# An RG-LRU and ternary-FFN layer: the first w1/w3 unit of the second sequence ahead of the first down product, a gate formed bank by bank, g's between scans

## The chip, the cores and the metric

The kernel runs on one core of a Trainium2 chip. The metric is the device time of one execution in microseconds, as the median of several runs. The engines have their own instruction streams: TensorE (PE, matmuls into PSUM; PEld is its weight load), VectorE (DVE), ScalarE (ACT), GpSimd (POOL) and SyncE (SP, which issues the DMAs here). They wait for each other by semaphores alone.

## The reference, cut to what matters

Two sequences of 512 tokens of width 256 go through one layer. The output is x plus a recurrent branch plus a feed-forward branch, both of the normalised x:

```python
xn = _layernorm(x, axis=-1)
# recurrent branch
y = gelu(xn @ w_y + b_y)
xb = xn @ w_x + b_x
conv = conv_b + sum(conv_w[k] * shifted(xb, k) for k in range(4))
gate_x = sigmoid(conv @ w_ig + b_ig)
gate_a = sigmoid(conv @ w_ag + b_ag)
log_a = -8.0 * gate_a * softplus(a_param)
a = exp(log_a); mult = sqrt(1.0 - exp(2.0 * log_a))
nx = gate_x * conv * mult            # first token: a = 0, mult = 1
h[t] = a[t] * h[t-1] + nx[t]         # scan over the 512 tokens
out1 = (h * y) @ w_out + b_out
# feed-forward branch, weights made ternary: w -> {-s, 0, s}, s = mean|w|
g = silu(xn @ w1q.T) * (xn @ w3q.T)  # hidden width 682 = 5 * 128 + 42
out2 = g @ w2q.T
return x + out1 + out2
```

## The kernel before, in words

Everything stays in SBUF. Channels lie on the partitions and tokens on the free axis; a sequence s is 512 columns, and 256 channels are two chunks c. Values that meet a matmul are split into a rounded part and its rest (hi and lo, kind fp32r), so a product of 128x512 is several matmuls: hi times hi, the weight's lo times hi, and hi times the value's lo. The order on each engine is written out by hand, and every engine does its list strictly in that order.

The recurrent branch comes first. TensorE forms the products with w_x (for the convolution), w_y, and the two gates WIG and WAG for s = 0 and 1. Gate products of a sequence lie in a slot of PSUM, which is two banks of 512 columns, one for each output chunk o. The slot of the second gate of sequence 0 (GA_SLOT[0] = 0) is that in which the w_x product of sequence 1 lay (X_SLOT[1] = 0), and older_taps(1, c) on VectorE (lines 484 to 496) reads bank c of it while it forms the convolution; conv_set counts finished convolutions, two for each sequence. Before that gate product TensorE waits for all four (line 780). dense_product (line 657) works chunk by chunk over both banks.

The feed-forward branch has ten units: hidden(n) for n = 0 to 9 (line 664), n = 5 * s + j, each with eight matmuls of 512 columns for w1 and w3 at once into a slot (H_SLOT), and hidden_tail for the 42 last channels of both sequences. For each unit, ScalarE forms silu_of(n) from the slot (line 327), VectorE g_of(n) = silu * s32 * the w3 half (line 508), ScalarE its rounded part g_hi_of(n) (line 335), GpSimd the rest, lo_of_g(n), which is called g_lo(n) here (line 253). The buffers of silu and g are rings of three. The tail has the same by tail_product, tail_hi (two casts, lines 567 and 568) and tail_lo (line 573), all on VectorE.

down(s, banks, first) (line 688) multiplies g with w2: for each j it waits for g_lo, does eight matmuls of 256 columns (four token tiles, hi and lo), and after the five j's comes the tail with four. project(s, first) (line 707) multiplies the gated scan with w_out, chunk by chunk, when hy_set says that gated_output(s, c) is done; its float32 matmuls are two records each in the trace, 32 records for both sequences. Both add into the same banks, for s = 0 down first and for s = 1 project first.

The recurrence on VectorE is, for each s: gated_input (line 518), squares, gated_products (line 529, once ScalarE has formed mult by a square root, line 370), scan(s, c) for the two chunks (line 536), gated_output(s, c) (line 541). threshold_2 (line 475) forms the scale and the threshold of w2 from a sum in PSUM. ScalarE changes its table before the square roots and again before the silus of sequence 1.

Five output steps (line 547) add x, and SyncE stores each.

Of the kernel before, what the change touches and what calls it, by code (L numbers as in the profile page):

```python
# [19 lines left out]
P = 128  # L20
# [5 lines left out]
KC = D // P  # L26
TILES = SEQ // P
FULL = HIDDEN // P
# [12 lines left out]
WX, WY, WIG, WAG, WOUT = range(5)  # L41


def build(nc: bass.Bass, x, dense, w13t, w2t, params, b_out, out):
# [7 lines left out]
    with ctx:  # L52
        def sb(name, shape, dt=f32):
            return ctx.enter_context(nc.sbuf_tensor(name, shape, dt))

        def sem(name):
            return ctx.enter_context(nc.semaphore(name))
# [9 lines left out]
        w_hi = sb("w_hi", [P, 5, KC, D], f32r)  # L67
        w_lo = sb("w_lo", [P, 5, KC, D], f32r)
# [7 lines left out]
        conv_hi = sb("conv_hi", [P, SEQS, KC, SEQ], f32r)  # L76
        conv_lo = sb("conv_lo", [P, SEQS, KC, SEQ], f32r)
# [39 lines left out]
        slot = [ctx.enter_context(nc.psum_tensor(f"slot{i}", [P, 2, SEQ], f32)) for i in range(4)]  # L117
        T_SLOT, X_SLOT, Y_SLOT = (0, 1), (2, 0), (3, 1)
        GX_SLOT, GA_SLOT = (2, 3), (0, 1)
# [13 lines left out]
        def xt_bank(s, h):  # L133
# [21 lines left out]
        w_lo_set = sem("w_lo_set")  # L155
# [7 lines left out]
        tap_set, tap_step, conv_set = sem("tap_set"), sem("tap_step"), sem("conv_set")  # L163
        conv_hi_set, conv_lo_set = sem("conv_hi_set"), sem("conv_lo_set")
        y_psum, y_set = sem("y_psum"), sem("y_set")
        gx_psum, ga_psum, tx_set, ta_set = sem("gx_psum"), sem("ga_psum"), sem("tx_set"), sem("ta_set")
        a_set, a2_set, mult_set, mult0_set = sem("a_set"), sem("a2_set"), sem("mult_set"), sem("mult0_set")
        nx_step, nx_set, h_set, hy_set = sem("nx_step"), sem("nx_set"), sem("h_set"), sem("hy_set")
        h_psum, silu_set, g_set, g_hi_set, g_lo_set = (
            sem("h_psum"), sem("silu_set"), sem("g_set"), sem("g_hi_set"), sem("g_lo_set"))  # L170
# [258 lines left out]
        def _(dve):  # L429
# [34 lines left out]
            def ternary_13():  # L464
                dve.wait_ge(thr_set, 2)
                dve.wait_ge(gaps_set, 1)
                parts = (slice(0, W3_AT), slice(W3_AT, W13))
                for i, cols in enumerate(parts):
                    nc.vector.tensor_scalar(below[:, :, cols], w13_raw[:, :, cols], thr[:, 1, i:i + 1], None, ALU.is_lt).then_inc(below_set, 1)
                for i, cols in enumerate(parts):  # L470
                    dve.wait_ge(below_set, i + 1)
                    nc.vector.scalar_tensor_tensor(out=w13_q[:, :, cols], in0=w13_raw[:, :, cols], scalar=thr[:, 0, i:i + 1],
                                                   in1=below[:, :, cols], op0=ALU.is_gt, op1=ALU.subtract).then_inc(w13_q_set, 1)

            def threshold_2():
                dve.wait_ge(sum2_psum, 1)
                nc.vector.tensor_scalar(scale[:, 2:3], sum2[:, 0:1], sum2[:, 1:2], 1.0 / WEIGHTS, ALU.add, ALU.mult).then_inc(s2_ready, 1)
                nc.vector.tensor_scalar(thr2[:, 0:1], sum2[:, 0:1], sum2[:, 1:2], 0.5 / WEIGHTS, ALU.add, ALU.mult).then_inc(s2_ready, 1)
                nc.vector.tensor_scalar(thr2[:, 1:2], sum2[:, 0:1], sum2[:, 1:2], -0.5 / WEIGHTS, ALU.add, ALU.mult).then_inc(s2_ready, 1)
                dve.wait_ge(s2_ready, 1)  # L480
                dve.wait_ge(thr_set, 3)
                nc.vector.tensor_tensor(s32[:, :], scale[:, 1:2], scale[:, 2:3], ALU.mult).then_inc(scale2_set, 1)
# [25 lines left out]
            def g_of(n):  # L508
                s, j = HJ[n]
                if n == 0:  # L510
                    dve.wait_ge(scale2_set, 1)
                dve.wait_ge(silu_set, n + 1)
                if n >= RING:
                    dve.wait_ge(g_lo_set, n - RING + 1)
                nc.vector.scalar_tensor_tensor(out=g[:, n % RING], in0=silu[:, n % RING], scalar=s32[:, 0:1],  # L515
                                               in1=slot[H_SLOT[s][j]][:, 1], op0=ALU.mult, op1=ALU.mult).then_inc(g_set, 1)

            def gated_input(s):

                dve.wait_ge(tx_set, KC * (s + 1))  # L520
                nc.vector.scalar_tensor_tensor(out=tx[:, s], in0=tx[:, s], scalar=1.0, in1=conv[:, s],
                                               op0=ALU.add, op1=ALU.mult).then_inc(nx_step, 1)
# [6 lines left out]
            def gated_products(s):  # L529

                dve.wait_ge(mult0_set, 1)
                dve.wait_ge(nx_step, s + 1)
                dve.wait_ge(mult_set, KC * (s + 1))
                nc.vector.tensor_tensor(tx[:, s], tx[:, s], mult[:, s], ALU.mult).then_inc(nx_set, 1)

            def scan(s, c):

                dve.wait_ge(nx_set, s + 1)
                nc.vector.tensor_tensor_scan(tx[:, s, c], ta[:, s, c], tx[:, s, c], 0.0, ALU.mult, ALU.add).then_inc(h_set, 1)

            def gated_output(s, c):

                dve.wait_ge(y_set, KC * s + c + 1)
                dve.wait_ge(h_set, KC * s + c + 1)
                nc.vector.tensor_tensor(tx[:, s, c], tx[:, s, c], y[:, s, c], ALU.mult).then_inc(hy_set, 1)
# [53 lines left out]
            older_taps(1, 1)  # L599
            threshold_13()  # L600
            ternary_13()
            gated_input(0)
            threshold_2()
            ternary_w2()
            squares(0)
            squares(1)
# [9 lines left out]
            gated_products(0)  # L616
            scan(0, 0)
            scan(0, 1)
            gated_output(0, 0)
            gated_output(0, 1)  # L620
            gated_products(1)
            g_of(5)
            scan(1, 0)
            g_of(6)
            scan(1, 1)
            gated_output(1, 0)
            g_of(7)
            gated_output(1, 1)
            g_of(8)
            g_of(9)  # L630
            for n in range(len(O_ALL)):
                output(n)

# [2 lines left out]
        def _(pe):  # L636
# [27 lines left out]
            def hidden(n):  # L664

                s, j = HJ[n]
                for o, col in enumerate((j * P, W3_AT + TAIL + j * P)):
                    for c in range(KC):
                        for v in (xt_hi, xt_lo):
                            mm = nc.tensor.matmul(slot[H_SLOT[s][j]][:, o], w13_q[:, c, col:col + P], v[:, s, c],  # L670
                                                  start=(c == 0 and v is xt_hi), stop=(c == KC - 1 and v is xt_lo))
                mm.then_inc(h_psum, 1)
# [10 lines left out]
            def out_tile(s, i, t):  # L683

                at = (t - O_TILES[s][i].start) * D
                return O_BANK[s][i][:, at:at + D]

            def down(s, banks, first):

                for j in range(FULL + 1):  # L690
                    if j < FULL:
                        pe.wait_ge(g_lo_set, FULL * s + j + 1)
                    else:
                        pe.wait_ge(gt_hi_set, 2)
                        pe.wait_ge(gt_lo_set, 1)
                        pe.wait_ge(b_placed, 32)
                    for i in banks:
                        tiles = O_TILES[s][i]
                        for t in tiles:
                            rows = slice(t * P, (t + 1) * P)  # L700
                            parts = (g_hi[:, j], g_lo[:, j]) if j < FULL else (gt,)
                            for k, v in enumerate(parts):
                                mm = nc.tensor.matmul(out_tile(s, i, t), v[:, s, rows], w2_q[:, j], start=(first and j == 0 and t == tiles.start and k == 0),  # L703
                                                      stop=(not first and j == FULL), skip_group_check=True)
                return mm
# [63 lines left out]
            dense_terms(slot[X_SLOT[1]], WX, [(w_hi, xt_lo[:, 1])], False, True).then_inc(xb_psum, 1)  # L769
            dense_product(slot[Y_SLOT[1]], WY, xt_hi[:, 1], xt_lo[:, 1], y_psum)  # L770

            def gate_product(s, m, slots, done, between=None):
                pe.wait_ge(w_lo_set, m + 1)
                dense_product(slot[slots[s]], m, conv_hi[:, s], conv_lo[:, s], done,
                              (conv_hi_set, KC * s + 1), (conv_lo_set, KC * s + 1), between)

            pe.wait_ge(conv_set, KC)
            gate_product(0, WIG, GX_SLOT, gx_psum)
            sums_of_w13()
            pe.wait_ge(conv_set, 2 * KC)  # L780
            gate_product(0, WAG, GA_SLOT, ga_psum)
            pe.wait_ge(thr_set, 3)
            gate_product(1, WIG, GX_SLOT, gx_psum, sum_of_w2)
            pe.wait_ge(y_set, 2 * KC)
# [11 lines left out]
            hidden(3)  # L796
            pe.wait_ge(g_set, 2)
            hidden(4)
            pe.wait_ge(w2_q_set, 1)
            pe.wait_ge(g_t_set, 1)  # L800
            down(0, range(len(O_TILES[0])), True)
            pe.wait_ge(g_set, 3)
            hidden(5)
            pe.wait_ge(g_set, 4)
            hidden(6)
            pe.wait_ge(g_set, 5)
# [8 lines left out]
            for i in range(len(O_TILES[1])):  # L815
                down(1, [i], False).then_inc(o_psum, 1)
# [27 lines left out]
```

## Time and profile before

| | us |
|---|---|
| median of 3 runs | 77.18 (77.08 to 77.36) |
| profiled execution | 77.82 |
| its span, first to last instruction | 76.0 |
| TensorE matmul busy | 70.0 (92%) |
| VectorE busy | 60.8 (80%) |
| ScalarE busy | 49.9 (66%) |
| GpSimd busy | 33.4 (44%) |

The granted TensorE clock is 1.000 (of 2.4 GHz) over the span. The times in the profile count from the first instruction. Busy shares are averages over the whole span; the stage rows and the timeline rows below tell more. A timeline row shows when an instruction started and how long it lasted, and this includes time in which it had started and was held up. In the name of a tile buffer numbers are left out, and tiles that share memory carry the name of the first: g and silu lie in w_raw there, ternary weights are w_q, y lies in xn_y.

### The profile page before, as it was taken

What the parts mean: (1) busy time and instruction counts of PE and PEld (TensorE: products, weight loads), DVE (VectorE), ACT (ScalarE), POOL (GpSimd) and SP (SyncE); (2) the same over time, 40 slices, a digit from 0 to 9 for tenths busy, and PEclk for the clock granted to TensorE, in tenths of its full rate; (3) what the DMA queues carried; (4) which work ended last, traced back from release to release, by engine and by line L of the source; (5) the groups of instructions that cost most, each with busy time, mean ns of one, the idle gap of its engine ahead of it and who ended that gap; (6) DMA issues with size and microseconds to landing.
All of it is one profiled execution on the core that took longest, in us unless ns stands there. A gap on an engine that the chain in (4) does not pass through costs nothing.

```text
span 76.0 us, 1062 instructions
## 1 busy us (share of the span) xinstructions
PE 70.0 (92%) x364; PEld 60.1 (79%) x364; DVE 60.8 (80%) x99; ACT 49.9 (66%) x76; POOL 33.4 (44%) x43
## 2 busy tenths in 40 slices
PE   4999879999999799999999999499999999999960
PEld 4999768877887678888888889388888888899950
DVE  4887599999999999999989999169999999400340
ACT  3663714899999999999989768996357429100000
POOL 6385646336661750052007968940007818910000
DMA  0989999910000000000000000000000000340062
GB/s 13 259 212 338 349 405 367 361 67 9 0 0 0 4 0 0 0 0 0 5 1 0 0 9 0 0 0 0 0 0 0 0 0 0 111 165 9 0 207 69
DMA packets 5095, 5.63 MB, mean 74 GB/s; under 512 B 525, under 2 KB 4578, under 8 KB 5090
## 3 DMA queue, kind: packets, MB, share of 16 engines
q1 hardware_dynamic: 4946, 5.55, 21.8%
q8 instruction: 3, 0.05, 0.2%
q10 hardware_dynamic: 144, 0.01, 0.1%
q14 instruction: 2, 0.02, 0.1%
HBM read 4.51 MB, written 1.05 MB: 73 GB/s over the span
## 4 chain that ended last, share of the span: by engine, by line
PE 37%; ACT 33%; DVE 9%; DMA 7%; issue 5%; POOL 3%; SPq 3%; DVEq 0%; ACTq 0%
PE slot L670 12%; PE slot L703 11%; PE slot L714 9%; DMA x_sb<-x 7%; ACT ta L363 4%; POOL g_lo L256 3%; ACT tx L349 3%; ACT conv_hi L342 3%; ACT xn_y L324 3%; PE slot L653 2%; ACT ta L355 2%; SPq L186 2%; ACT g_hi L300 2%; DVE w_raw L515 2%; DVE stats L437 2%
## 5 line engine op out<-in xcount | busy, mean ns | idle before, releaser
L256 POOL TENSOR_TENSOR g_lo<-w_raw,g_hi 128x512 fp32r<-128x512 f32 x10 | 15.9, 1609 | 16.1 <-ACT g_hi L338 16.1
L670 PE MATMUL slot<-xt_lo,w_q 128*128 128x512 f32 x40 | 15.7, 394 | 0.0
L670 PE MATMUL slot<-xt_hi,w_q 128*128 128x512 f32 x40 | 15.7, 393 | 0.0
L703 PE MATMUL slot<-w_q,g_hi 128*128 128x256 f32 x40 | 10.2, 292 | 1.1 <-POOL g_lo L256 1.1
L703 PE MATMUL slot<-w_q,g_lo 128*128 128x256 f32 x40 | 9.8, 282 | 0.0
L332 ACT ACTIVATE w_raw<-slot,scale 128x512 f32<-128x512 f32 x10 | 6.8, 686 | 4.3 <-PE slot L670 4.3
L493 DVE SCALAR_TENSOR_TENSOR conv<-slot,par,conv 128x511 f32<-128x511 f32 (+2 forms) x12 | 9.0, 748 | 0.4
L703 PEld LDWEIGHTS slot<-w_q,g_hi 128*128 128x128 f32 x40 | 7.6, 191 | 1.6 <-POOL g_lo L256 1.6
L670 PEld LDWEIGHTS slot<-xt_lo,w_q 128*128 128x128 f32 x40 | 7.5, 188 | 1.7
L670 PEld LDWEIGHTS slot<-xt_hi,w_q 128*128 128x128 f32 x40 | 7.5, 188 | 1.7
L338 ACT ACTIVATE g_hi<-w_raw 128x512 fp32r<-128x512 f32 x10 | 6.3, 630 | 3.4 <-DVE w_raw L515 3.2
L552 DVE TENSOR_TENSOR x_sb<-slot,x_sb 128x512 f32<-128x512 f32 (+1 forms) x5 | 2.8, 581 | 6.8 <-PE slot L703 6.8
L703 PEld LDWEIGHTS slot<-w_q,g_lo 128*128 128x128 f32 x40 | 7.6, 191 | 0.1
L515 DVE SCALAR_TENSOR_TENSOR w_raw<-w_raw,s,slot 128x512 f32<-128x512 f32 x10 | 7.2, 740 | 0.4 <-ACT w_raw L332 0.4
L226 POOL TENSOR_TENSOR w_lo<-w_raw,w_hi 128x512 fp32r<-128x512 f32 x4 | 5.1, 1287 | 4.6 <-ACT w_hi L283 4.6
L722 PE MATMUL slot<-ones 128*128 128x128 f32 x28 | 6.2, 420 | 1.0 <-POOL ones L214 1.0
L714 PE MATMUL slot<-w_raw,tx 128*128 128x256 f32 x32 | 7.1, 379 | 0.0
L653 PE MATMUL slot<-conv_hi,w_hi 128*128 128x512 f32 x16 | 6.4, 401 | 0.5 <-DVE conv L493 0.5
L251 POOL TENSOR_TENSOR conv_lo<-conv,conv_hi 128x512 fp32r<-128x512 f32 x4 | 5.4, 1343 | 3.4 <-ACT conv_hi L342 3.4
L722 PEld LDWEIGHTS slot<-ones 128*128 128x128 f32 x28 | 6.0, 330 | 1.0 <-POOL ones L214 1.0
L714 PEld LDWEIGHTS slot<-w_raw,tx 128*128 128x128 f32 x32 | 6.1, 190 | 0.9
L653 PE MATMUL slot<-conv_hi,w_lo 128*128 128x512 f32 x16 | 6.3, 394 | 0.0
(105 smaller groups left out, 143.1 us busy)
## 6 DMA issues: line engine op xcount, KB each, us to landing
w_raw<-w13t SPq DMA_DIRECT2D x2, 682.0 KB, 8.1
w_raw<-dense SPq DMA_DIRECT2D x5, 256.0 KB, 5.7
out<-x_sb SPq DMA_DIRECT2D x3, 256.0 KB, 2.2
w_raw<-w2t SPq DMA_DIRECT2D x1, 640.0 KB
x_sb<-x SPq DMA_DIRECT2D x4, 128.0 KB, 2.2
x_sb<-x SPq DMA_DIRECT2D x1, 512.0 KB, 5.4
out<-x_sb SPq DMA_DIRECT2D x2, 128.0 KB, 1.7
w_raw<-w2t SPq DMA_DIRECT2D x2, 42.0 KB
```

The lines of the kernel that those rows point to most:

```text
L226: nc.gpsimd.tensor_tensor(w_lo[:, m], w_raw[:, m], w_hi[:, m].bitcast(f32), ALU.subtract).then_inc(w_lo_set, 1)
L251: nc.gpsimd.tensor_tensor(conv_lo[:, s, c], conv[:, s, c], conv_hi[:, s, c].bitcast(f32), ALU.subtract).then_inc(conv_lo_set, 1)
L256: nc.gpsimd.tensor_tensor(g_lo[:, j, s], g[:, n % RING], g_hi[:, j, s].bitcast(f32), ALU.subtract).then_inc(g_lo_set, 1)
L332: nc.scalar.activation(silu[:, n % RING], slot[H_SLOT[s][j]][:, 0], ACT.Silu, scale=scale[:, 0:1]).then_inc(silu_set, 1)
L338: nc.scalar.activation(g_hi[:, j, s], g[:, n % RING], ACT.Copy).then_inc(g_hi_set, 1)
L493: nc.vector.scalar_tensor_tensor(out=conv[:, s, c, i:], in0=slot[X_SLOT[s]][:, c, 0:SEQ - i], scalar=par[:, CONV_W + KC * k + c:CONV_W + K ...
L515: nc.vector.scalar_tensor_tensor(out=g[:, n % RING], in0=silu[:, n % RING], scalar=s32[:, 0:1], in1=slot[H_SLOT[s][j]][:, 1], op0=ALU.mult ...
L653: mm = nc.tensor.matmul(dst[:, o], w[:, m, c, o * P:(o + 1) * P], v[:, c], start=(first and i == 0 and c == 0), stop=(last and i == len(te ...
L670: mm = nc.tensor.matmul(slot[H_SLOT[s][j]][:, o], w13_q[:, c, col:col + P], v[:, s, c], start=(c == 0 and v is xt_hi), stop=(c == KC - 1 a ...
L703: mm = nc.tensor.matmul(out_tile(s, i, t), v[:, s, rows], w2_q[:, j], start=(first and j == 0 and t == tiles.start and k == 0), stop=(not ...
L714: mm = nc.tensor.matmul(out_tile(s, i, t), tx[:, s, c, t * P:(t + 1) * P], w_raw[:, WOUT, c], start=(first and c == 0 and t == tiles.start ...
L722: nc.tensor.matmul(slot[WARM_SLOT][:, 0, 0:P], ones[:, :], ones[:, :], start=True, stop=True)
```

## The change

There are four edits. On TensorE, hidden(5) comes before down(0) and no longer after it. The second gate of sequence 0 is formed bank by bank by a new function, gate_bank, which waits for three convolutions ahead of bank 0 and for four ahead of bank 1. The first down product takes the tail before its last j. On VectorE, threshold_2 comes before gated_input(0), and the g's of sequence 1 are put between gated products, scans and gated outputs, with gated_output(1, 0) and (1, 1) at the end.

```diff
@@ VectorE @@
             threshold_13()
             ternary_13()
+            threshold_2()
             gated_input(0)
-            threshold_2()
             ternary_w2()
...
             gated_products(0)
             scan(0, 0)
             scan(0, 1)
+            g_of(5)
+            gated_products(1)
+            g_of(6)
             gated_output(0, 0)
+            g_of(7)
             gated_output(0, 1)
-            gated_products(1)
-            g_of(5)
             scan(1, 0)
-            g_of(6)
+            g_of(8)
             scan(1, 1)
+            g_of(9)
             gated_output(1, 0)
-            g_of(7)
             gated_output(1, 1)
-            g_of(8)
-            g_of(9)
@@ TensorE @@
             def down(s, banks, first):
-                for j in range(FULL + 1):
+                order = (*range(FULL - 1), FULL, FULL - 1) if first else range(FULL + 1)
+                for j in order:
...
+            def gate_bank(s, m, slots, o):
+                terms = [(w, v, c) for w, v in ((w_hi, conv_hi), (w_lo, conv_hi), (w_hi, conv_lo)) for c in range(KC)]
+                for i, (w, v, c) in enumerate(terms):
+                    mm = nc.tensor.matmul(slot[slots[s]][:, o], w[:, m, c, o * P:(o + 1) * P], v[:, s, c],
+                                          start=(i == 0), stop=(i == len(terms) - 1))
+                return mm
...
-            pe.wait_ge(conv_set, 2 * KC)
-            gate_product(0, WAG, GA_SLOT, ga_psum)
+            pe.wait_ge(w_lo_set, WAG + 1)
+            for o in range(KC):
+                pe.wait_ge(conv_set, KC + o + 1)
+                mm = gate_bank(0, WAG, GA_SLOT, o)
+            mm.then_inc(ga_psum, 1)
...
             hidden(4)
+            pe.wait_ge(g_set, 3)
+            hidden(5)
             pe.wait_ge(w2_q_set, 1)
             pe.wait_ge(g_t_set, 1)
             down(0, range(len(O_TILES[0])), True)
-            pe.wait_ge(g_set, 3)
-            hidden(5)
```

## Rows read from the trace of the kernel before

**Rows 1.** Stages: us, busy (x instructions) of PE, PEld, DVE, ACT, POOL, clock, DMA.
```profile
45.00:52.00 7.00, 5.86 (x46) 5.45 (x45) 4.71 (x6) 6.60 (x9) 4.90 (x3) 1.00 0.00 0
52.00:61.00 9.00, 9.00 (x41) 7.29 (x40) 9.00 (x10) 4.50 (x7) 3.27 (x2) 1.00 0.00 0
```
**Rows 2.** The chain of waits that ended last: start us, us, what.
```profile
46.72 2.30 POOL g_lo L256
...
52.01 9.26 PE slot L670 x40
```
**Rows 3.** Timeline, TensorE at its two waits: start us, us, instruction, idle before and releaser.
```profile
24.34 0.28 PE L736 MATMUL slot<-abs_sum,ones 128*128 128x2 f32 x2
25.15 0.50 PE L653 MATMUL slot<-conv_hi,w_hi 128*128 128x512 f32 x1 [0.53 <-DVE conv L493]
...
49.07 0.38 PE L703 MATMUL slot<-w_q,g_hi 128*128 128x256 f32 x1 [1.11 <-POOL g_lo L256]
```
**Rows 4.** TensorE, first and last: 24 of down(0), 40 of hidden(5) to (9), projections.
```profile
44.92 0.28 PE L703 MATMUL slot<-w_q,g_hi 128*128 128x256 f32 x1
...
47.67 0.28 PE L703 MATMUL slot<-w_q,g_lo 128*128 128x256 f32 x1
...
51.85 0.40 PE L670 MATMUL slot<-xt_hi,w_q 128*128 128x512 f32 x1
...
60.88 0.39 PE L670 MATMUL slot<-xt_lo,w_q 128*128 128x512 f32 x1
61.11 7.07 PE L714 MATMUL slot<-w_raw,tx 128*128 128x256 f32 x32
```
**Rows 5.** ScalarE: silu_of(3) and g_hi_of(2).
```profile
43.27 0.69 ACT L332 ACTIVATE w_raw<-slot,scale 128x512 f32<-128x512 f32 x1 [0.52 <-PE slot L670]
43.85 0.62 ACT L338 ACTIVATE g_hi<-w_raw 128x512 fp32r<-128x512 f32 x1
```
**Rows 6.** VectorE: g_of(2), the two casts of the tail, and tail_lo.
```profile
42.86 0.75 DVE L515 SCALAR_TENSOR_TENSOR w_raw<-w_raw,s,slot 128x512 f32<-128x512 f32 x1
43.64 0.83 DVE L567 CAST gt_hi<-w_raw 42x1024 fp32r<-42x1024 f32 x1
44.51 0.69 DVE L568 CAST gt<-w_raw 42x1024 fp32r<-42x1024 f32 x1
...
46.67 1.22 DVE L573 TENSOR_TENSOR gt<-w_raw,gt_hi 42x1024 fp32r<-42x1024 f32 x1
```
**Rows 7.** GpSimd: g_lo(0) and (1), g_lo(2), g_lo(3) and (4).
```profile
40.45 3.47 POOL L256 TENSOR_TENSOR g_lo<-w_raw,g_hi 128x512 fp32r<-128x512 f32 x2 [5.73 <-ACT g_hi L338]
44.55 1.81 POOL L256 TENSOR_TENSOR g_lo<-w_raw,g_hi 128x512 fp32r<-128x512 f32 x1 [0.63 <-ACT g_hi L338]
46.72 3.54 POOL L256 TENSOR_TENSOR g_lo<-w_raw,g_hi 128x512 fp32r<-128x512 f32 x2 [0.36 <-ACT g_hi L338]
```
**Rows 8.** VectorE: gated_output(0,0) and (0,1); scan(1,0), g_of(6), scan(1,1), gated_output(1,0).
```profile
53.63 1.27 DVE L545 TENSOR_TENSOR tx<-tx,xn_y 128x512 f32<-128x512 f32 x2
...
56.61 1.22 DVE L539 TENSOR_TENSOR_SCAN tx<-ta,tx 128x512 f32<-128x512 f32 x1
57.74 0.72 DVE L515 SCALAR_TENSOR_TENSOR w_raw<-w_raw,s,slot 128x512 f32<-128x512 f32 x1
58.38 1.61 DVE L539 TENSOR_TENSOR_SCAN tx<-ta,tx 128x512 f32<-128x512 f32 x1
59.92 1.72 DVE L545 TENSOR_TENSOR tx<-tx,xn_y 128x512 f32<-128x512 f32 x1
```
**Rows 9.** GpSimd: g_lo(5) and g_lo(6).
```profile
57.43 1.48 POOL L256 TENSOR_TENSOR g_lo<-w_raw,g_hi 128x512 fp32r<-128x512 f32 x1 [7.18 <-ACT g_hi L338]
59.21 1.88 POOL L256 TENSOR_TENSOR g_lo<-w_raw,g_hi 128x512 fp32r<-128x512 f32 x1 [0.30 <-ACT g_hi L338]
```
**Rows 10.** gated_products(0) on VectorE, and ScalarE's table load before silu_of(5).
```profile
50.08 1.25 DVE L534 TENSOR_TENSOR tx<-tx,mult 128x1024 f32<-128x1024 f32 x1 [2.19 <-ACT mult L370]
...
51.20 1.28 ACT L332 ACT_TABLE_LOAD   x1
```

## The prediction

> **What bounds the kernel now.** I read the stage table first. TensorE is busy for the whole of 52 to 61 us and VectorE is too; only 45 to 52 us has TensorE time missing (5.86 of 7 us), at a granted clock of 1.00 [rows 1]. The chain of waits then says which of the two sets the end: from 52.01 us it is TensorE alone, first 9.26 us of w1/w3 units [rows 2], then projections and the last down product. So before the change TensorE ends last, and VectorE, as busy, is a step behind it. How far behind is what matters here: the scanned output of the second sequence (gated_output(1,0), called hy3 below) is ready at 59.92 + 1.72 = 61.64 us [rows 8], while project(1), which reads it, begins at its place 17 of 32 records from 61.11 us, 61.11 + 16 x 0.2155 = 64.56 us (0.2155 is (67.8 - 61.11)/31, 7.07 us for 32 records less the 0.38 us that one lasts) [rows 4]. VectorE has 2.9 us of slack there, and nothing else reaches the end by another way.
>
> TensorE's own idle time is in two places: 0.53 us before the second gate product of the first sequence, and 1.11 us before j = 3 of the first down product, which waits for GpSimd's g_lo(3) [rows 3].
>
> **Part 1, the gate bank by bank.** The wait for all four convolutions becomes one for three, then four. The last record of the sums starts at about 24.45 us (two of them, 0.28 us long, from 24.34) and the gate could not start before 25.15, where its first record also lasts 0.50 us in place of the usual 0.39 [rows 3, 4]. After the change the six products of bank 0 start at about 24.68; bank 1 then wants the fourth convolution 1.4 us later, when it is long there. The same 12 matmuls, nothing added: TensorE is s = 0.58 us earlier from here. I bound s by 0.4 (the wait alone, less queueing) and 0.65. It survives to the w1/w3 units because threshold_2 goes ahead of gated_input(0): without that the constants that hidden(0) waits for would come a gated_input later, some 1.2 us (the same shape takes 1.25 [rows 10]); the two steps only change places, so their own cost on VectorE is nil (0 to 0.1).
> ScalarE gets nothing from s for now: it works through its own list without a gap that TensorE causes until silu(3), which waited 0.52 us for it at 43.27 us [rows 5].
>
> **Part 2, hidden(5) before down(0).** Eight matmuls of 0.2315 us ((60.88 - 51.85)/39) are 1.85 us [rows 4]. With s, hidden(5) runs 44.33 to 46.18, down(0) starts there, and its first 24 products (0.1196 us each, (47.67 - 44.92)/23 [rows 4]) end at 49.05. If g_lo(3) still came at 49.02 [rows 2] and g_lo(4) at 50.26 [rows 7], both waits would be gone (the tail's four products now lie before j = 4), hidden(6) would start at 51.45 in place of 53.70, and project(1) at 62.3.
>
> **Part 3, where that collides.** g_lo(3) will not come at 49.02. The rows show that a VectorE instruction with two inputs in SBUF, or a cast from SBUF to SBUF, and a GpSimd tensor_tensor never run together: the later one waits to the end of the other. Three cases: g_lo(6) starts at 59.21, the scan ends at 59.99, g_lo(6) ends 1.10 us after that; gated_output(1,0) is next on VectorE at 59.92 but GpSimd was waiting first, so it ends 0.55 us after g_lo(6) (alone it takes 0.67) [rows 8, 9]. g_lo(3) starts 0.05 us behind tail_lo (46.67 + 1.22 = 47.89) and ends 1.13 us after it [rows 2, 6]. And cast 1 of the tail (43.64) stands until g_lo(1) is through at 43.92, ends at 44.47; cast 2 follows at 44.51, g_lo(2) at 44.55, 0.04 us late, and it waits for the cast until 45.20 [rows 6, 7].
> That last race turns. silu(3) comes up to s earlier, so g_hi(2) starts when g_of(2) is done (42.86 + 0.75, and 0.04) and not at 43.85, where silu(3) let it in [rows 5, 6]; g_lo(2) asks at 43.65 + 0.62 + 0.08 = 44.35, while cast 1 runs, and is first at 44.48. It ends at 45.63, cast 2 at 46.19 in place of 45.20. VectorE is 0.99 us late, and with it g_of(3), g_of(4), tail_lo, ScalarE's g_hi(4), table load and four square roots, and gated_products(0), which starts at 51.07 in place of 50.08 [rows 10]. An s of 0.05 us is enough for this, so its bounds do not matter. g_lo(3) ends at 50.00, g_lo(4) at 51.24: TensorE waits 1.0 us before j = 3 after all, j = 3 and the tail run to 51.59, j = 4 to 52.55. hidden(6) to hidden(9) are 32 x 0.2315 = 7.41, to 59.96; project(0), 3.45, to 63.41. TensorE is 1.15 us ahead of before.
>
> **Part 4, VectorE's new order.** It now has g_of(8) and g_of(9) ahead of hy3. A step starts 0.08 us before the one ahead of it ends, so undisturbed it adds to that end: gated_products 1.14 (1.22 or 1.25 long), scan 1.13, g_of 0.66, gated_output 0.60 [rows 8, 10]. Behind a GpSimd hold a scan ends 1.08 after it (58.38 + 1.61 against 57.43 + 1.48), a gated_output 0.55 [rows 8, 9]. GpSimd asks 0.04 + 0.63 + 0.08 = 0.75 us after each g_of ends. That is what makes the spread order dear: behind every g_of stands a VectorE step that needs the shared access, and g_lo lands on it. I walk it.
> scan(0,0), scan(0,1) end at 54.70 (silu(5) is there at 54.17, its table loaded 0.99 late [rows 10]). g_of(5) to 55.35. gated_products(1) to 56.49; g_lo(5) asks at 56.09, gets 56.49 to 57.60. g_of(6) to 57.15; gated_output(0,0) waits to 57.60, ends 58.15. g_lo(6) asks at 57.89, holds to 59.27. g_of(7) to 58.81; gated_output(0,1) ends at 59.82. g_lo(7) asks at 59.59 (its g_hi stands behind silu(8), which ends at 58.98), before scan(1,0) does (59.74), holds to 60.94; scan(1,0) ends at 62.02. g_of(8) to 62.68; scan(1,1) to 63.81, which g_lo(8) waits for and holds to 64.90. g_of(9) to 64.47; gated_output(1,0) ends at 64.90 + 0.55 = 65.45: hy3. g_lo(9) comes before gated_output(1,1), which ends at 67.12; project(1) wants that one 8 x 0.2155 after its start, 67.2 us.
> TensorE is ready at 63.41, so it waits 2.1 us and starts project(1) at 65.50 where it was 64.56, with about 0.1 us for the first product after a wait (0.38 us at 49.07 for one of 0.28 [rows 3, 4]). Sum: +0.94 + 0.10 = +1.0 us. Everything behind it is as before: g_lo(9) at 66.6 is long there when the last down product comes to it, and the stores of the first sequence are issued by 68.5 us, four us ahead of the last.
> The bounds of this step: the walk holds 2.3 us of collisions ahead of hy3 (0.4, 0.4, 1.1, 0.4); with none of them hy3 comes at 63.2, TensorE is not held, and the change is worth -1.15; with one more collision than I count (1.1 us) +2.1. I take the walk, since each of its waits repeats one in the rows. The new waits stall no other queue: ScalarE's silu(9) is done at 60.84, no DMA is moved.
>
> The Trainium skill ("SBUF — State Buffer", on the two sides of SBUF) says that VectorE and GpSimd share a port pair as an exclusive lock, that an instruction with two SBUF inputs or in a two-port mode takes it, and that who starts first keeps it for the whole instruction. It also names the intuition it replaces, bandwidth shared in proportion. By the lock the walk stands; by sharing, overlaps would stretch both sides a little and the time would lie nearer the no-collision end. The trace agrees with the lock: 1.72 us for a 0.67 us step, ending 0.55 after the other's end [rows 8, 9].
>
> **From the profile's time to the median.** The profiled run took 77.82 us for a span of 76.0; the median of the runs is 77.18, so I add the difference of spans, 1.0, to 77.18: **78.2 us**.
>
> **Rivals.**
> A. The forecast, +1.0: chance 0.52. Its own range is 77.8 to 78.7.
> B. g_lo(7) asks just after scan(1,0). The margin is 0.15 us (59.59 against 59.74), and it hangs on silu(8), which waits for TensorE. The scan then runs first, gated_output(1,0) ends at 64.75, project(1) starts at 64.80: +0.24 + 0.10 = +0.3, 77.5 us. Chance 0.14.
> C. The race at 44.5 us does not turn (the g_lo(2) request comes later than I work out by 0.16 us). Then everything on VectorE is 0.99 earlier, with the same collisions: hy3 at 64.45, project(1) at 64.50, TensorE idle from 62.3: -0.06 + 0.10, 77.2 us, no change. Chance 0.14.
> D. The other side: TensorE stays the bound. Its mechanism is the refilled stall and s, at the price of -1.15 us with the race turned (76.0) and -2.3 without (74.9). It decides from the point where VectorE has hy3 before 64.1 us: that is faster by 0.5%, and it wants the collisions ahead of hy3 to cost under 0.9 us and not 2.3 (under 1.9 if the race doesn't turn). For it: the kernel before paid only 1.5 us in all there (0.40 on scan(1,1), 1.05 on gated_output(1,0) [rows 8]), and had 2.9 us of slack. Against it: the new order puts a locked step behind each of the five g_of's. Chance 0.20.
>
> **How the numbers follow.** A change of 0.5% (0.39 us) is about what a measurement of this kernel tells from none. Slower by more: A and a little of B, 0.54. Within: most of B, and C, 0.25. Faster: D and the edge of C, 0.21. The range reaches from D's first value, 76.0, to 78.6; outside are D without the race (about 0.08) and a further collision (0.08).
>
> **What would show it.** Right: gate products start near 24.7 us; silu(3) without a wait; g_lo(2) about 1.15 us long from cast 1's end and cast 2 over 1.5 us long; no TensorE gap at hidden(5), one of about 1 us before j = 3; VectorE with both gated outputs of sequence 0 and scan(1,0) lengthened; a TensorE gap of about 2 us before project(1), and a chain of waits that runs through VectorE and GpSimd in 55 to 65 us. Wrong: a project(1) that follows project(0) without a gap (D), or cast 2 at 0.69 us (C). A granted clock under 1.00 behind the longer gap would add to A; no gap in the trace of before is that long.

## The result, and the profile after

| | before | changed |
|---|---|---|
| median (range), us, 4 runs each | 77.25 (77.08 to 77.36) | 79.62 (78.85 to 79.78) |
| ratio, 95% interval | | 1.029 (1.022 to 1.036) |
| profiled execution, its span | 77.82, 76.0 | 79.61, 77.8 |
| granted clock of the changed kernel's 4 executions | | 1.000, 0.978, 1.000, 0.978 |

The changed kernel is 2.9% slower. The forecast was slower, 78.2 us, with an upper end of 78.6: the direction came as forecast, the size did not. Three more sets of six executions on other occasions gave ratios of 1.015, 1.020 and 1.022; what differs between them is shown below. (Ratios set aside executions over 1.5% above the fastest of their kernel, which here took out neither of the two with a low clock; wherever a low clock matters, I give all executions.)

The stages of the profile after, columns as in [rows 1]: TensorE now has its hole in 61 to 68 us (4.92 of 7), while VectorE is busy for all of it.

```profile
45.00:52.00 7.00, 6.01 (x43) 5.47 (x42) 4.71 (x6) 5.02 (x7) 4.81 (x3) 1.00 0.01 2
52.00:61.00 9.00, 9.00 (x46) 7.55 (x45) 8.96 (x10) 6.84 (x11) 3.79 (x3) 1.00 0.00 0
61.00:68.00 7.00, 4.92 (x23) 4.05 (x22) 7.00 (x7) 1.73 (x3) 3.48 (x3) 1.00 0.00 0
```

Everything in this trace is 0.57 us late from the start, since the statistics of the second sequence waited longer for the load of x. VectorE's timeline at that place, before and after:

```profile
8.49 0.43 DVE L437 BATCH_NORM_STATS2 stats<-x_sb 128x6 f32<-128x256 f32 x1 [1.06 <-DMA x_sb<-x]
```
```profile
9.06 0.75 DVE L437 BATCH_NORM_STATS2 stats<-x_sb 128x6 f32<-128x256 f32 x2 [1.53 <-DMA x_sb<-x]
```

Take 0.57 off and the lines can be laid beside the forecast. The gate products start right behind the sums:

```profile
25.06 0.71 PE L777 MATMUL slot<-conv_hi,w_hi 128*128 128x512 f32 x2
```

That is 24.49 on the old clock where it was 25.15, so s is 0.66 us (forecast 0.58, bound 0.65). The race of [rows 5 to 7], ScalarE, VectorE and GpSimd after the change:

```profile
44.24 0.63 ACT L338 ACTIVATE g_hi<-w_raw 128x512 fp32r<-128x512 f32 x1 [0.32 <-DVE w_raw L515]
```
```profile
44.24 0.82 DVE L567 CAST gt_hi<-w_raw 42x1024 fp32r<-42x1024 f32 x1
45.09 1.72 DVE L568 CAST gt<-w_raw 42x1024 fp32r<-42x1024 f32 x1
```
```profile
44.95 1.30 POOL L256 TENSOR_TENSOR g_lo<-w_raw,g_hi 128x512 fp32r<-128x512 f32 x1 [0.45 <-ACT g_hi L338]
```

It turned: g_lo(2) asks at 44.38 on the old clock (forecast 44.35), goes first, and cast 2 takes 1.72 us for its 0.69. VectorE's list behind it, then GpSimd's g_lo(5) to g_lo(8) (compare [rows 8, 9]):

```profile
57.03 0.74 DVE L515 SCALAR_TENSOR_TENSOR w_raw<-w_raw,s,slot 128x512 f32<-128x512 f32 x1
57.69 1.13 DVE L545 TENSOR_TENSOR tx<-tx,xn_y 128x512 f32<-128x512 f32 x1
58.74 0.73 DVE L515 SCALAR_TENSOR_TENSOR w_raw<-w_raw,s,slot 128x512 f32<-128x512 f32 x1
59.40 1.12 DVE L545 TENSOR_TENSOR tx<-tx,xn_y 128x512 f32<-128x512 f32 x1
60.45 2.29 DVE L539 TENSOR_TENSOR_SCAN tx<-ta,tx 128x512 f32<-128x512 f32 x1
62.66 0.72 DVE L515 SCALAR_TENSOR_TENSOR w_raw<-w_raw,s,slot 128x512 f32<-128x512 f32 x1
63.30 1.21 DVE L539 TENSOR_TENSOR_SCAN tx<-ta,tx 128x512 f32<-128x512 f32 x1
64.43 0.72 DVE L515 SCALAR_TENSOR_TENSOR w_raw<-w_raw,s,slot 128x512 f32<-128x512 f32 x1
65.07 1.05 DVE L545 TENSOR_TENSOR tx<-tx,xn_y 128x512 f32<-128x512 f32 x1
```
```profile
56.72 1.55 POOL L256 TENSOR_TENSOR g_lo<-w_raw,g_hi 128x512 fp32r<-128x512 f32 x1 [4.84 <-ACT g_hi L338]
58.52 1.46 POOL L256 TENSOR_TENSOR g_lo<-w_raw,g_hi 128x512 fp32r<-128x512 f32 x1 [0.24 <-ACT g_hi L338]
60.22 1.44 POOL L256 TENSOR_TENSOR g_lo<-w_raw,g_hi 128x512 fp32r<-128x512 f32 x1 [0.24 <-ACT g_hi L338]
64.12 1.46 POOL L256 TENSOR_TENSOR g_lo<-w_raw,g_hi 128x512 fp32r<-128x512 f32 x1 [2.46 <-ACT g_hi L338]
```

Both gated outputs of sequence 0 are 0.45 us too long, scan(1,0) 1.1, gated_output(1,0) 0.4: the four collisions of the forecast, at its sizes (a collision is a step held up because the other engine of the two is using their shared access). hy3 ends at 66.12 - 0.57 = 65.55 (forecast 65.45). On TensorE that leaves these two waits (compare [rows 3, 4]):

```profile
50.67 0.39 PE L704 MATMUL slot<-w_q,g_hi 128*128 128x256 f32 x1 [0.98 <-POOL g_lo L256]
...
60.58 3.61 PE L715 MATMUL slot<-w_raw,tx 128*128 128x256 f32 x16
66.27 3.69 PE L715 MATMUL slot<-w_raw,tx 128*128 128x256 f32 x16 [2.08 <-DVE tx L545]
```

project(1) starts at 65.70 on the old clock where it was 64.56. From the start of the second sequence's statistics to the end of the span it is 68.7 us, and 67.5 before: **the change costs 1.2 us in the trace, and 0.57 is the start.** The two profiled executions are 1.8 us apart; the other 0.6 of the 2.4 us between the medians is that the one of before, 77.82, lies 0.6 above its median.

### The profile page after: what moved, and what is told of

The parts are those of the page before. It is cut to its first block, busy times and chain, and to the rows that moved or that the text cites. A ratio compares the mean times of both kernels' runs of the same rounds, so it can differ in the third digit from the quotient of the medians.

```text
span 77.8 us, 1062 instructions
## 1 busy us (share of the span) xinstructions
PE 69.8 (90%) x364; PEld 59.9 (77%) x364; DVE 63.8 (82%) x99; ACT 49.9 (64%) x76; POOL 33.1 (42%) x43
## 4 chain that ended last, share of the span: by engine, by line
ACT 33%; DVE 22%; PE 16%; issue 12%; DMA 8%; SPq 3%; POOL 2%; DVEq 0%; ACTq 0%
DMA x_sb<-x 8%; PE slot L704 7%; DVE tx L539 6%; DVE w_raw L515 5%; PE slot L715 5%; ACT ta L363 3%; ACT tx L349 3%; ACT conv_hi L342 3%; ACT xn_y L324 3%; PE slot L653 2%; ACT ta L355 2%; DVE gt L568 2%; SPq L186 2%; ACT g_hi L300 2%; DVE tx L545 2%
## 5 line engine op out<-in xcount | busy, mean ns | idle before, releaser
L539 DVE TENSOR_TENSOR_SCAN tx<-ta,tx 128x512 f32<-128x512 f32 x4 | 5.8, 1484 | 0.0
L545 DVE TENSOR_TENSOR tx<-tx,xn_y 128x512 f32<-128x512 f32 x4 | 5.0, 1265 | 0.0
```

## The experiments

Medians are of all executions of a label; "low" counts those with a mean granted clock below 0.99; "behind x" is the span less the start of the second sequence's statistics, in the profiled execution; it has no meaning where that step was moved (e4 to e6, e8, e9), and v2_again is given by its time alone. b0 is the kernel before itself, and its interval leaves out 1.000, so an interval here can be off by some tenths of a per cent.

| kernel | median (range), us | low | ratio | behind x |
|---|---|---|---|---|
| b0_before_again | 77.28 (76.63 to 78.03) | 0 of 12 | 0.994 (0.990 to 0.998) | 67.5 |
| a0_after_again | 79.07 (78.28 to 79.82) | 2 of 6 | 1.015 (1.009 to 1.021) | 68.7 |
| a1_after_third | 79.67 (78.73 to 80.35) | 3 of 6 | 1.020 (1.013 to 1.027) | 68.7 |
| a2_after_fourth | 79.09 (78.72 to 80.47) | 2 of 6 | 1.022 (1.015 to 1.028) | 68.7 |
| e1_old_g_order | 77.69 (77.41 to 78.44) | 0 of 12 | 1.004 (1.000 to 1.008) | 68.0 |
| e2_new_g_order_alone | 78.37 (78.08 to 78.96) | 0 of 6 | 1.011 (1.006 to 1.016) | 68.9 |
| e3_no_seq1_rest | 76.44 (75.96 to 77.00) | 0 of 6 | 0.988 (0.982 to 0.994) | 66.5 |
| e7_gate_bank_alone | 79.28 (78.24 to 80.85) | 3 of 6 | 1.013 (1.007 to 1.019) | 70.0, low |
| v1_cast_by_dma | 76.11 (76.01 to 76.49) | 0 of 6 | 0.984 (0.979 to 0.989) | 66.5 |
| v2_output_before_scan | 75.38 (74.67 to 76.15) | 0 of 6 | 0.971 (0.963 to 0.979) | 65.6 |
| v2_again | 75.46 (75.01 to 76.47) | 0 of 6 | 0.975 (0.969 to 0.981) | |
| e4_start_uncoupled | 79.73 (79.53 to 79.78) | 0 of 6 | 1.030 (1.024 to 1.035) | |
| e6_uncoupled_before | 79.69 (79.61 to 79.81) | 0 of 6 | 1.029 (1.025 to 1.034) | |
| e5_change_uncoupled | 81.59 (80.62 to 82.62) | 3 of 6 | 1.043 (1.037 to 1.049) | |
| e9_uncoupled_again | 81.52 (80.74 to 82.38) | 3 of 6 | 1.044 (1.037 to 1.051) | |
| e8_uncoupled_filler | 80.63 (80.57 to 80.65) | 0 of 6 | 1.042 (1.037 to 1.047) | |
| a3_after_look | 80.06 | 1 of 1 | | 70.4, low |
| e10_uncoupled_look | 80.79 | 0 of 1 | | |

### Both kernels again

> The kernel before once more, unchanged, beside the others on one chip. What is open: the result was 1.4 us above my forecast, while the two traces put project(1) only 1.14 us later once the start is taken off (the second sequence's x, a 512 KB load, landed 0.57 us later in the changed kernel's trace, and everything behind it is later by that). Theory START: the load's landing varies from run to run by some 0.6 us, in either kernel, and the runs of before happened to lie low. Expects times from 77.0 to 77.9 here, and a trace whose bn_stats of the second sequence start between 7.9 and 9.1 us. Rival LAYOUT: the changed program itself makes the load slower. Expects all times within 77.0 to 77.4 and the early landing here in every run.

> The changed kernel once more, unchanged. LOCK theory (my forecast's mechanism, as the trace shows it): hy3 ends 1.1 us later than project(1) started before; ratio to before about 1.014 once the start is the same. START expects a ratio between 1.012 and 1.022 over many runs, with times spread over 0.7 us. LAYOUT expects about 1.030 again, with the bn_stats of the second sequence starting at 9.0 us or later.

The statistics of the second sequence started at 7.66 us here in the kernel before and at 7.76 in the changed one, where LAYOUT wanted 9.0 or later. Behind x both traces repeat to 0.1 us: an execution's time less that start is 69.33 and 69.29 us in the two traces of before and 70.50 to 70.55 in the four of the changed kernel at full clock. With these and a3's 72.15 for a low clock, the times give a mean start of 8.3 us over 69 executions of before and 8.1 over 23 of the changed kernel (an estimate). So LAYOUT falls, although the ratios of a1 and a2 below, 1.020 and 1.022, are what it asked for. The kernel before ranged over 76.6 to 78.8 us in its 69 executions, median 77.48; the four of the first result, 77.08 to 77.36, all lay below that median.

### VectorE's list, and TensorE's edits, each alone

In e1 the lines between scan(0, 1) and output(n) stand as before the change:
```diff
-            g_of(5)
-            gated_products(1)
-            g_of(6)
             gated_output(0, 0)
-            g_of(7)
             gated_output(0, 1)
+            gated_products(1)
+            g_of(5)
             scan(1, 0)
...
```


> The changed kernel with VectorE's list behind tail_lo as it was before (gated outputs of sequence 0 first, g_of(8) and g_of(9) last); the TensorE edits and threshold_2 stay. LOCK expects the race of cast 2 and g_lo(2) still turned (cast 2 about 1.7 us long, gated_products(0) about 1.0 us late), but g_of(5) later: hidden(8) waits for g_set 6 about 1.4 us. By the same walk project(1) starts at 64.9 on the clock of the trace of before, +0.4 us, ratio 1.005. Rival ORDER-IS-FREE (VectorE's order costs nothing and the TensorE edits themselves cost the time): ratio as the changed kernel's.

e2 is that diff's reverse, put on the kernel before.

> The kernel before with only VectorE's new list behind tail_lo. LOCK expects the race not turned (cast 2 0.69 us, gated_products(0) at its old place), collisions on gated_output(0,0) and (0,1) of 0.4 us each, but silu(8) later than in the changed kernel since TensorE is not ahead, so scan(1,0) takes its turn before g_lo(7): hy3 at 64.7, project(1) +0.2 to +0.4 us, ratio 1.003 to 1.005. If g_lo(7) comes first all the same: +1.0, 1.013. Rival TE-ONLY (the time was lost by TensorE's edits, by the turned race alone): ratio 1.000.

e1: +0.5 us behind x, and a new wait on TensorE where it was expected, for g_of(5):
```profile
57.08 0.50 PE L670 MATMUL slot<-xt_hi,w_q 128*128 128x512 f32 x1 [1.34 <-DVE w_raw L515]
```
Cast 2 took 1.71 us, and ORDER-IS-FREE falls. The ratio alone, 1.004, would not tell this kernel from the one before; the 0.5 us rests on the trace. So TensorE's edits without the new list cost 0.5 us, the list without them 1.4, and both together 1.2: each half loses alone, and they do not add up. e2 missed: I expected +0.2 to +0.4, or +1.0 if g_lo(7) came ahead of scan(1,0), and behind x it was +1.4. Its ratio, 1.011, is near the 1.013 of that second branch by luck, for scan(1,0) did go first (59.59 against 59.68 us). Its VectorE timeline says why it was late:
```profile
53.55 0.75 DVE L515 SCALAR_TENSOR_TENSOR w_raw<-w_raw,s,slot 128x512 f32<-128x512 f32 x1 [0.91 <-ACT w_raw L332]
54.22 1.22 DVE L534 TENSOR_TENSOR tx<-tx,mult 128x1024 f32<-128x1024 f32 x1
55.41 0.75 DVE L515 SCALAR_TENSOR_TENSOR w_raw<-w_raw,s,slot 128x512 f32<-128x512 f32 x1
56.07 1.74 DVE L545 TENSOR_TENSOR tx<-tx,xn_y 128x512 f32<-128x512 f32 x1
```
```profile
55.97 1.30 POOL L256 TENSOR_TENSOR g_lo<-w_raw,g_hi 128x512 fp32r<-128x512 f32 x1 [6.79 <-ACT g_hi L338]
```
hidden(5) still came late there, so ScalarE had silu(6) late too and g_hi(5) stands behind it in its list; g_lo(5) asked just before gated_output(0,0), which then stood for the whole of it. I had g_lo(5) behind gated_products(1). The lock was right, my order of requests was not.

### The collisions taken away

> The changed kernel with GpSimd's five g_lo's of the second sequence cut from 512 to 8 columns; the other columns are set to zero once, at about 35 us, so this part of the computation (the rests of g of sequence 1) is left out. TensorE multiplies as many columns as before. LOCK: the collisions of 56 to 65 us shrink to almost nothing, VectorE has hy3 at 63.2 us on the clock of the trace of before, project(1) follows project(0) without a gap at 63.4, so about 2.2 us ahead of the changed kernel and 1.1 ahead of before: ratio 0.985 to 0.990. Cast 2 still about 1.7 us long. Rival VECTOR-WORK (VectorE is late by the amount of its work, not by collisions): hy3 stays within 0.5 us of the changed kernel's, ratio above 1.008.

```diff
+                cols = slice(0, SEQ) if n < FULL else slice(0, 8)
-                nc.gpsimd.tensor_tensor(g_lo[:, j, s], g[:, n % RING], g_hi[:, j, s].bitcast(f32), ALU.subtract).then_inc(g_lo_set, 1)
+                nc.gpsimd.tensor_tensor(g_lo[:, j, s, cols], g[:, n % RING, cols], g_hi[:, j, s, cols].bitcast(f32), ALU.subtract).then_inc(g_lo_set, 1)
...
+            nc.gpsimd.memset(g_lo[:, :, 1, 8:].bitcast(f32), 0.0).then_inc(lo_zero, 1)
```
It is 2.2 us less behind x than the changed kernel, hy3 comes at 63.18 on the old clock (forecast 63.2), and project(1) follows without a gap. VectorE's four gated outputs in this kernel, by their source line (min/median/max ns):
```profile
L548 DVE TENSOR_TENSOR tx<-tx,xn_y x4: 680/682/683, 56.8 to 62.8; 128x512 f32<-128x512 f32 x4
```
and in the changed one:
```profile
L545 DVE TENSOR_TENSOR tx<-tx,xn_y x4: 1052/1126/1756, 57.7 to 66.0; 128x512 f32<-128x512 f32 x4
```
VECTOR-WORK falls: VectorE's work is the same in both.

### The race taken away, then one collision

v1: the second cast leaves VectorE; SyncE copies the rounded rows instead.
```diff
-                nc.vector.tensor_copy(gt[0:TAIL]..., g_t[HALF:HALF + TAIL]).then_inc(gt_hi_set, 1)
...
+            sp.wait_ge(gt_hi_set, 1)
+            sp.dma_start(gt[0:TAIL].bitcast(f32), gt_hi[HALF:HALF + TAIL].bitcast(f32)).then_inc(gt_copied, 16)
...
-                        pe.wait_ge(gt_hi_set, 2)
+                        pe.wait_ge(gt_copied, 16)
```


> The changed kernel with the tail's second cast taken off VectorE: a DMA copies the rounded rows (the same values) from gt_hi to gt. LOCK: the race has no loser any more. gated_products(0) at 49.4 in place of 51.1 us on the clock of the trace of before, TensorE's stall before j = 3 gone, project(0) at 58.9; but the new order's collisions stay, hy3 at 63.5: project(1) 1.0 us ahead of before and 2 us ahead of the changed kernel, ratio 0.986 to 0.992. Rival RACE-IS-SMALL (the turned race costs nothing at the end): ratio as the changed kernel's, 1.012 to 1.015.

v2 is v1 with gated_output(1, 0) ahead of scan(1, 1), and g_of(9) last:
```diff
             g_of(8)
-            scan(1, 1)
-            g_of(9)
             gated_output(1, 0)
+            scan(1, 1)
             gated_output(1, 1)
+            g_of(9)
```


> v1_cast_by_dma with the last steps on VectorE in the order scan(1,0), g_of(8), gated_output(1,0), scan(1,1), gated_output(1,1), g_of(9). LOCK: hy3 at 61.3 us and hy4 at 64.1 on the clock of the trace of before, both in time for a project(1) at 62.3; TensorE is the bound again, 2.2 us ahead of before: ratio 0.970 to 0.976. If a collision more lands on scan(1,1): hy4 one us late, ratio 0.984.

> v2_output_before_scan again on another chip: ratio 0.970 to 0.978 and no run with a low clock, since its longest gap on TensorE behind 20 us is under 0.5 us.

v1 came at 0.984, just below its range, with the wait in down(0) gone and one left before project(1):
```profile
62.85 3.69 PE L717 MATMUL slot<-w_raw,tx 128*128 128x256 f32 x16 [1.07 <-DVE tx L548]
```
Behind x it is 2.2 us shorter than the changed kernel (66.5 against 68.7), so RACE-IS-SMALL falls. But not all of that is the race. At gated_products(0) v1 is 1.76 us ahead, of which the forecast gives 1.0 to the race and 0.7 is the cast itself, which VectorE no longer does. The other 0.5 comes after it: scan(1,0) now starts just ahead of g_lo(7), the order of rival B, and is not held up. VectorE, then GpSimd:
```profile
57.73 1.21 DVE L542 TENSOR_TENSOR_SCAN tx<-ta,tx 128x512 f32<-128x512 f32 x1
```
```profile
57.81 2.19 POOL L259 TENSOR_TENSOR g_lo<-w_raw,g_hi 128x512 fp32r<-128x512 f32 x1 [0.55 <-ACT g_hi L341]
```
v2 is 2.9% and, on another chip, 2.5% faster than the kernel before, and TensorE no longer waits before project(1). hy3 ends at 61.15 us on the old clock and gated_output(1,1), called hy4, at 64.16 (forecast 61.3 and 64.1). It gained 1.9 us behind x and not 2.2: g_lo(8) still met scan(1,1) (2.29 us for 1.21), and inside project(1) TensorE waited for hy4, which made the projections 0.4 us longer:
```profile
58.27 7.44 PE L717 MATMUL slot<-w_raw,tx 128*128 128x256 f32 x32
```
That is 7.44 us for the 7.07 of [rows 4].

### The start taken out

e4 is the kernel before, e5 the changed one, with one step moved; e6 is e4 and e9, e10 are e5 again.
```diff
+            xt_lo_of(0)
             dve.wait_ge(x_loaded[TILES], 16)
             statistics(1, range(TILES))
             variance(1, range(TILES))
-            xt_lo_of(0)
```


> The kernel before with one step moved at the start of VectorE's list: xt_lo_of(0) ahead of the wait for the second sequence's x and its statistics. START (the time of a run follows the landing of that 512 KB load, which varies by 1.4 us between traces, because TensorE's first products wait for xt_lo_of(0) behind it): the runs of this kernel spread over less than 0.8 us where those of before spread over 1.4 (76.6 to 78.6), with a median within 0.4 us of before. Rival OTHER-SPREAD (the spread comes from somewhere else, the clock or the stores): the same spread as before.

> The changed kernel with the same moved step as e4_start_uncoupled, whose six runs lay within 0.25 us. Beside it on one chip, the pair gives the price of the change without the varying start. LOCK with START: 1.2 us longer than e4_start_uncoupled (as the traces give from the start of the second sequence's statistics to the end, 68.7 against 67.5 us), so 80.9 us, a ratio of 1.015 between the two, each with a spread under 0.4 us. Rival MORE (the first result's 2.4 us is the change's own): 82.1 us, 1.03.

> e4_start_uncoupled once more, for the comparison on one chip: 79.5 to 79.8 us.

e4's six runs lie within 0.25 us, e6's within 0.20, so START holds: the spread of the kernel before is the landing of that load. The median is 2.2 us higher, where I had expected it within 0.4. Two waits on TensorE are new: 1.26 us for GpSimd's w_lo of WY, which stands in GpSimd's list behind a reciprocal root that starts at 11.27 us in place of 10.46, and 0.68 us for a later xt_lo. For the comparison it does not matter, since e5 has both too. e5 against e6 on one chip: 80.62, 80.80, 80.85 at clock 1.000, which is +1.1 us on 79.69 (LOCK), and 82.34, 82.41, 82.62 at clock 0.979. So MORE is right of half of the executions, and these are the ones with the low clock.

### The gate bank alone, and the clock

> The kernel before with only the gate formed bank by bank and threshold_2 ahead: TensorE 0.58 us earlier, nothing else. LOCK: the race of cast 2 and g_lo(2) turns (cast 2 about 1.7 us), g_lo(3) comes at 50.0 on the clock of the trace of before, while TensorE reaches j = 3 at 47.2: a stall of 2.8 us, j = 4 at 51.3, down(0) ends at 52.8 in place of 51.8. VectorE has slack enough behind it. So an edit that only starts TensorE earlier makes the kernel 1.0 us slower: ratio 1.011 to 1.014. Rival PLAIN (0.58 us earlier is 0.58 us gained, or lost in the stall that is there anyway): ratio 0.992 to 1.000.

It takes the gate_bank and threshold_2 parts of the change and no others. Three executions at clock 1.000 took 78.24 to 78.73 us, about 1 us more than before (ratio 1.013), and cast 2 took 1.71 us, as the race says: TensorE started earlier and the kernel became slower, so PLAIN falls. The two parts were not tested apart. The other three executions were 79.82 to 80.85 us at a low clock (0.978, 0.957, 0.978), and the profiled one is of these. TensorE's wait, and the windows behind it:
```profile
49.56 0.39 PE L703 MATMUL slot<-w_q,g_hi 128*128 128x256 f32 x1 [2.79 <-POOL g_lo L256]
```
```profile
50.00:51.00 1.00, 0.97 (x8) 0.77 (x7) 0.42 (x1) 1.00 (x3) 0.76 (x1) 0.97 0.00 0
51.00:52.00 1.00, 1.00 (x6) 1.00 (x7) 0.97 (x2) 0.98 (x3) 0.00 (x0) 0.50 0.00 0
```
The seventh column of numbers behind the window is the granted clock: it goes from 2.4 to 1.2 GHz at about 51 us, 1.4 us after the wait ended.

> e5_change_uncoupled with six small products of ones put on TensorE between the wait for g_of(8) and project(1), into a bank that nothing reads any more; they fill 2 us or so of the 2.1 us gap before project(1) and leave the result alone. CLOCK theory (behind the gap the granted clock falls to half in about half of the runs, 10 of 22 so far, and that costs 1.6 us): no run of this kernel below 0.99, all within 0.5 us of each other near 80.8 us. Rival CLOCK-ELSEWHERE (the low clock comes from another place, such as the gap before j = 3 or the bank by bank products): still some runs at 0.978 and 82.4 us.

```diff
+FILL = 6
...
             pe.wait_ge(g_set, 9)
+            for _ in range(FILL):
+                nc.tensor.matmul(slot[1][:, 1, 0:P], ones[:, :], ones[:, :], start=True, stop=True)
             project(1, True)
```


> e5_change_uncoupled once more, as the other half of the comparison. CLOCK: two groups, near 80.8 us at clock 1.000 and near 82.4 at 0.979, about half of the runs in each; if the profiled run is of the second, its clock is half in a stretch of 3 to 4 us that begins after the gap before project(1), and all before it is as in the first.

> The changed kernel, unchanged, a third time. START: its times less 1.2 us fall within those of before in the same call, 76.6 to 78.6, ratio 1.015 with an interval of some 0.006. LAYOUT: its times less 1.2 us lie above the median of before again, ratio 1.02 or more.

> The changed kernel a fourth time, for a trace of its low-clock execution, which none of the three so far is. CLOCK: as e9, on top of the start's spread: 78.2 to 79.6 at clock 1.000 and 1.7 us more at 0.978.

> The changed kernel, one look, for a trace of an execution with a low clock (7 or so in 10 that one of the two looks has it). CLOCK: if the clock is 0.978, it is half from project(1) on, behind the 2.1 us gap, and 1.00 before it, also behind the 1.0 us gap in down(0).

> e5_change_uncoupled, one look, for the same: 80.8 us at clock 1.000, or 82.4 us at 0.979 with half the clock from project(1) on.

e8: 80.57 to 80.65 us, six of six at clock 1.000, where e9 had 80.74, 80.76, 80.76 and 82.27, 82.28, 82.38 (three at 0.979). The 0.9 us wait in down(0) is still in e8, so CLOCK-ELSEWHERE has little left: at e9's rate of one half, six full clocks in a row would come by chance once in 64. The filler took 1.5 us and not 2, and left a wait of 0.73:
```profile
65.07 1.50 PE L828 MATMUL slot<-ones 128*128 128x128 f32 x12
67.30 3.69 PE L716 MATMUL slot<-w_raw,tx 128*128 128x256 f32 x16 [0.73 <-DVE tx L546]
```
a1, a2 and a0 are the changed kernel: 7 of 18 low. START missed in a1: its times less 1.2 us reach 79.15, above the 78.6 it allowed. The three that reach so far are the three at a low clock, and the other three stay within it. Of the two single executions, e10 was at 1.000 (80.79 us) and a3 at 0.978 (80.06 us). a3's TensorE and windows:
```profile
49.46 0.39 PE L704 MATMUL slot<-w_q,g_hi 128*128 128x256 f32 x1 [0.92 <-POOL g_lo L256]
...
65.05 5.38 PE L715 MATMUL slot<-w_raw,tx 128*128 128x256 f32 x16 [2.08 <-DVE tx L545]
```
```profile
64.00:65.00 1.00, 0.00 (x0) 0.00 (x0) 1.00 (x2) 0.59 (x1) 0.68 (x2) 1.00 0.00 0
65.00:66.00 1.00, 0.95 (x4) 0.91 (x5) 1.00 (x1) 0.00 (x0) 1.00 (x1) 0.90 0.00 0
66.00:67.00 1.00, 1.00 (x3) 0.72 (x3) 1.00 (x2) 0.00 (x0) 0.02 (x1) 0.50 0.00 0
67.00:68.00 1.00, 1.00 (x4) 0.80 (x3) 0.77 (x2) 0.00 (x0) 0.00 (x0) 0.50 0.00 0
68.00:69.00 1.00, 1.00 (x4) 0.81 (x3) 0.00 (x0) 0.00 (x0) 0.00 (x0) 0.50 0.86 285
69.00:70.00 1.00, 1.00 (x5) 0.83 (x5) 0.00 (x0) 0.00 (x0) 0.00 (x0) 0.89 0.72 240
```
The clock stays full behind the 0.92 us wait and falls behind the 2.08 us one; project(1) takes 5.38 us for 3.69. 1.7 us is the price, also behind x (70.4 against 68.7), and the two groups of e9 have 1.5 to 1.6. Without the uncoupled start it is blurred: the changed kernel's 13 executions at full clock have a median of 78.84 and its 10 low ones of 79.87.

## Why the prediction was right and wrong

**The mechanism, with its sizes: right.** s, the turned race, the 1.0 us wait in down(0), the four collisions ahead of hy3, g_lo(7) ahead of scan(1,0), 2.1 us idle before project(1): each is in the trace within 0.1 us of the walk, but for the start of project(1), which is 0.2 later; in all +1.2 us in place of +1.0. e3, e7 and e1, forecast with the same walk, came at their ratios, v1 just below its own; e2 did not follow it. The lock that the Trainium skill's page "SBUF — State Buffer" (on the two sides of SBUF) describes is what the traces show, 680 ns against 1052 to 1756 for one step.

**The step that failed: what the 2.1 us gap does to the clock.** I had written the gap down and said that a clock under 1.00 "would add to A; no gap in the trace of before is that long", and then gave it no price, no rival and no place in the range, whose upper end of 78.6 left room for A alone. Runs: 10 of 23 executions of the changed kernel have a low mean clock, and the one of them with a trace, a3, shows it halved behind that gap, at 1.7 us; none of 69 of the kernel before is below 0.995. Among the four of the first result it is two. Without those falls they would have been 79.61, 78.85, 78.1 and 77.9 us, a median of 78.5 (an estimate, 1.7 off each of the two), inside the range and 0.3 from the forecast: the clock is 1.1 of the 1.4 us by which the forecast was short. That was a rival of its own: half of the executions at +1.0, half at +2.7.

**The step from the trace to the median: wrong by the start.** I added a difference of spans to a median of three runs. The profiled execution, 77.82 against 77.08 to 77.36, showed already that one program varies by 0.7 us; the range had nothing for it. Of the four executions, the profiled one has no low clock and is 79.61 us, by a late landing (9.06 us; others of this kernel 7.76 to 8.32). The median I added to was low too, 77.18 against 77.48 of 69. Over all executions the two medians are 77.48 and 79.44, +2.0 us, and +1.4 with the full clock alone.

**Rivals.** B and C did not come in any trace of the changed kernel; B's order came in e2, v1 and v2, so its margin of 0.15 us was as thin as the prediction says. D's condition (collisions under 0.9 us) is what e3 made, and it is 1.0 us ahead of before where D says 1.15. v2, where the race is gone, still has 1.5 us of collisions ahead of hy3, under the 1.9 that D allows for that case, and is 1.9 ahead where D says 2.3.

## What to carry to other kernels

Walk the requests of VectorE and GpSimd for their shared access as a queue in time, step by step: in the kernel before, 0.04 us decided who asked first, and its turning moved 1 us; starting TensorE 0.66 us earlier made this kernel slower. When a forecast puts an idle gap on TensorE that is longer than any the trace has, price the fall of the clock behind it as a case of its own. And compare traces from a common event (here the landing of a load), since the start alone moved the total by more than the effect.

## What the hardware showed that I had not expected

- With a gap of 2.1 us on TensorE 16 of 36 executions (changed kernel, e5, e9, e10) had a low mean clock, with one of 2.8 us 3 of 6 (e7); in both kinds one trace shows the half clock behind the gap (a3, e7). With none over 1.4 us (e1, e2, v1) it was 0 of 24.
- GpSimd, once waiting, went ahead of VectorE's next instruction, though that one started 0.03 us after the one before it: so two VectorE steps in a row are parted by it (cast 1 ends at 45.06, cast 2 starts at 45.09 and takes 1.72 us, g_lo(2) had asked at 44.95).
- The statistics behind a load of x that runs beside others started between 7.41 us (without a wait for it) and 9.06 us in ten traces of the same transfers, and the time of the kernel followed one for one: less that start it was 70.50 to 70.55 us in four traces of the changed kernel.
